# Expert routing of a gated FFN kernel rewritten: ranks from two matmuls, 16-bit one-hots, tile 0 looked up first

## The reference

```python
# layer 1: E = 4, F = 512, VOCAB = 25000, Wg = Wu = Wd = ctx (4, 512, 512)
expert_ids = min(clip(token_ids, 0, VOCAB - 1) // 6250, 3)
for e in range(E):
    g = silu(einsum('bsd,fd->bsf', h, Wg[e]))
    u = einsum('bsd,fd->bsf', h, Wu[e])
    y = einsum('bsf,df->bsd', g * u, Wd[e])
    out = where((expert_ids == e)[..., None], y, out)
# layer 2
g = einsum('th,ih->ti', xf, gate_w) * gate_s
u = einsum('th,ih->ti', xf, up_w) * up_s
out = einsum('ti,hi->th', silu(g) * u, down_w) * down_s
# whole
x = x + tanh(g_xattn[0]) * layer1(layernorm(x))
x = x + tanh(g_ffn[0]) * layer2(layernorm(x))
```

## Time and profile before

| | |
|---|---|
| median of 3 runs | 418.86 us (418.78 to 419.2) |
| the profiled execution, its own time | 418.32 us |
| its span, first to last instruction | 416.5 us |
| busy: PE, DVE, ACT, POOL | 371.1, 249.7, 139.9, 98.7 us |
| mean granted clock of TensorE | 0.991 |
| DMA | 34.53 MB in 14957 packets |

### The profile page before, as it was taken

One profiled execution on the slowest core, in us unless ns is written; L12 is line 12 of the kernel. 1 busy time (PEld: TensorE's weight loads), 2 busy tenths in 40 slices (PEclk: granted clock), 3 DMA queues, 4 the chain that ended last, 5 costly groups with the idle time before them and its releaser, 6 DMA issues.

```text
span 416.5 us, 6049 instructions
## 1 busy us (share of the span) xinstructions
PE 371.1 (89%) x1740; PEld 304.0 (73%) x1740; DVE 249.7 (60%) x461; ACT 139.9 (34%) x240; POOL 98.7 (24%) x135
## 2 busy tenths in 40 slices
PE   0116999999999998999999999999999999999990
PEld 0015788888878876888888888788888888888870
DVE  6998788888887796744545424545425645322243
ACT  4502455454554533633222222322222322222220
POOL 4562445556544232000100200101200101200003
PEclk9999999999999999999999999999999999999996
DMA  7445455655442132530000130000130000100002
GB/s 266 150 133 171 137 146 186 181 169 201 136 170 76 50 127 100 181 126 2 0 2 0 76 126 1 0 0 0 76 126 0 0 0 3 75 23 0 0 2 102
DMA packets 14957, 34.53 MB, mean 83 GB/s; under 512 B 2400, under 2 KB 2400, under 8 KB 14944
## 3 DMA queue, kind: packets, MB, share of 16 engines
q1 hardware_dynamic: 10624, 20.21, 15.2%
q0 software_dynamic: 4320, 14.16, 9.9%
HBM read 25.19 MB, written 9.18 MB: 83 GB/s over the span
## 4 chain that ended last, share of the span: by engine, by line
PE 84%; DVE 9%; POOL 2%; issue 2%; DMA 1%; POOLq 0%; ACT 0%; DVEq 0%
PE bank L1032 38%; PE bank L922 22%; PE bank L1045 19%; PE bank L914 3%; PE bank L936 2%; DVE work L239 1%; DMA rows<-x,gidx 1%; DVE shifted L625 1%; POOL out L442 1%; DVE work L677 1%; DVE is_low L607 1%; POOL rstd L362 1%; DVE is_low L633 1%; DVE xn L650 0%; DMA ids_i<-ids 0%
## 5 line engine op out<-in xcount | busy, mean ns | idle before, releaser
L1032 PE MATMUL bank<-work,wgu 128*128 x704 | 166.8, 389 | 1.3 <-DVE work L677 1.3
L1032 PEld LDWEIGHTS bank<-work,wgu 128*128 128x128 f32 x704 | 132.1, 188 | 29.1 <-issue 1.6
L922 PE MATMUL bank<-work 128*128 x432 | 109.9, 404 | 3.6 <-DVE work L677 2.9
L922 PEld LDWEIGHTS bank<-work 128*128 128x128 f32 x432 | 79.8, 191 | 20.7 <-issue 4.8
L1045 PE MATMUL bank<-work,hp 128*128 128x512 f32 x352 | 88.2, 393 | 0.0
L807 DVE SCALAR_TENSOR_TENSOR sh<-bank,gs,sh 128x512 f32<-128x512 f32 (+1 forms) x45 | 33.1, 738 | 89.3 <-PE bank L1032 89.2
L1045 PEld LDWEIGHTS bank<-work,hp 128*128 128x128 f32 x352 | 65.1, 188 | 13.2 <-DVE hp L812 0.2
L511 ACT ACTIVATE sh<-bank,gs 128x512 f32<-128x512 f32 x44 | 30.3, 689 | 85.4 <-PE bank L1032 84.6
L515 ACT ACTIVATE hp<-sh 128x512 fp32r<-128x512 f32 (+1 forms) x45 | 28.0, 623 | 87.2 <-DVE sh L807 87.2
L812 DVE TENSOR_TENSOR hp<-sh,hp 128x512 fp32r<-128x512 f32 (+1 forms) x45 | 30.6, 680 | 30.1 <-ACT hp L515 30.0
L362 POOL TENSOR_TENSOR rstd<-ve,half 128x1 f32<-128x1 f32 x31 | 17.9, 577 | 128.6 <-DVE ve L644 128.5
(11 more groups left out here) (125 smaller groups left out, 251.4 us busy)
## 6 DMA issues: line engine op xcount, KB each, us to landing
raw<-guT SPq DMA_DIRECT2D x16, 352.0 KB
ctx_in<-ctxT SPq DMA_DIRECT2D x4, 1024.0 KB, 8.9
rows<-x_rows SPq DMA_DIRECT2D x8, 512.0 KB, 4.2
checked<-dwT SPq DMA_DIRECT2D x11, 256.0 KB, 3.0
rows<-dwT SPq DMA_DIRECT2D x11, 256.0 KB, 2.9
dsb<-down_s SPq DMA_DIRECT2D x1, 256.0 KB, 5.0
out<-rows,oidx POOLq DMA_INDIRECT x16, 2.7
rows<-x,inow POOLq DMA_INDIRECT x12, 3.6
```

The source lines that it names most:

```text
L922: mm = pe.matmul(out_ps[:, :], part(s)[:, c * P:(c + 1) * P], ctx_w(e, c, w), start=n == 0, stop=n == last)
L1032: mm = pe.matmul(out_ps[:, :], wgu[:, row + h, w, c * P:(c + 1) * P], moving, start=n == 0, stop=n == last)
```

## The change

- The bounds are compared in one integer operation with a table. The running counts `seen` go to PE as they are, and two accumulated matmul groups give each token's rank and the experts' counts; rounding up to tiles is done by adding a large constant (`ROUND`). The experts' gaps are added in three steps (`slots`).
- The one-hots are 16-bit throughout, with the column index innermost, compared against tables that POOL makes (`minus_j`, `tile_of`). PE looks tile 0 up first, with one column (`token_0`), and its gather starts on a semaphore of its own; the table of the other tiles follows.
- The second lookup goes. Instead POOL scatters the 2048 token numbers by rank into DRAM, sixteen indirect DMAs of 128 words, placed between the gathers, and SP loads `oidx` from there, after the checked rows and ahead of the MLP's first rows.
- All sixteen `ctx_lo` are DVE's. ACT does expert 3's rounding after x_hi(0), and the tanh of the gates after x_hi(1).
- PE waits for the high part before the first pass of a product, for the low part before the second, and in steps 0 to 3 for the weights' rest before the third. Tile 0 always belongs to expert 0.
- The checks stand beside steps 6 to 16, and the maximum follows step 16.

```diff
-POOL_LO = 5
-POOL_LO_NEXT = 7
-POOL_LO_LATE = 14
+ROUND = 1.5 * 2 ** 30
+CHECK_AT = 6
+FIRST = 2
...
+    by_rank = nc.dram_tensor("token_by_rank", [TOKENS, 1], U32).ap()
...
-            sp.wait_ge(S["x_landed"], 16)
...
+            sp.wait_ge(first_landed[FIRST - 1], 16)
             sp.dma_start(dsb[:, :], down_s.partition_broadcast(P)).then_inc(S["small_in"], 16)
-
+            sp.wait_ge(S["x_landed"], 16)
...
+            checks_from = CHECK_AT + RAWS
+            with sp.Fori(RAWS, checks_from) as q:
                 next_piece(q)
-                c, c_before, c_checked = sp.snap(q - 2), sp.snap(16 * (q - 2)), sp.snap(q - 2)
+            with sp.Fori(checks_from, PIECES) as q:
+                next_piece(q)
+                before_q = CHECK_AT + RAWS - 2
+                c, c_before, c_checked = (sp.snap(q - before_q), sp.snap(16 * (q - before_q)),
+                                          sp.snap(q - before_q))
                 sp.wait_ge(S["check_landed"], c_before)
                 hold(sp)
                 sp.wait_ge(S["bits_done"], c_checked)
                 hold(sp)
                 check_row(c)
-            with sp.Fori(RAWS + IC - 2, PIECES) as q:
-                next_piece(q)
-
+            for c in range(2 + PIECES - checks_from, IC):
+                sp.wait_ge(S["check_landed"], 16 * c)
+                sp.wait_ge(S["bits_done"], c)
+                check_row(c)
+            sp.wait_ge(S["ranked"], 16 * CT)
+            sp.dma_start(oidx[:, :], by_rank.rearrange("(t p) o -> p (t o)", p=P),
+                         allow_slow_non_contiguous=True)\
+              .then_inc(S["oidx_ready"], 16)
...
+            pool.iota(minus_j[:, :, :], pattern=[[-1, P], [0, CT]], base=0, channel_multiplier=0, **exact)\
+                .then_inc(S["consts"], 1)
...
+            def place_tokens(c_from, c_to):
+                for c in range(c_from, c_to):
+                    pool.indirect_dma_start(
+                        by_rank, bass.IndirectOffsetOnAxis(ap=rank_i[:, c:c + 1], axis=0),
+                        token_i[:, c:c + 1], None).then_inc(S["ranked"], 16)
...
-            for n in range(POOL_LO):
-                ctx_lo(pool, n)
...
+            pool.wait_ge(S["first_ready"], 1)
+            gather(ring_slot(0), gidx[:, 0:1], first_landed[0])
             pool.wait_ge(S["tables_ready"], 1)
-            for k in range(5):
-                if k:
-                    pool.wait_ge(S["x_landed"], 16 * k)
-                gather(ring_slot(k), gidx[:, k:k + 1])
-                if k == 0:
-                    for n in range(POOL_LO, POOL_LO_NEXT):
-                        ctx_lo(pool, n)
-                if k == 1:
-                    inverse_std(0)
-                if k == 2:
-                    for n in range(POOL_LO_LATE, EXPERTS * KC):
-                        ctx_lo(pool, n)
-                    inverse_std(1)
+            gather(ring_slot(1), gidx[:, 1:2], first_landed[1])
+            gather(ring_slot(2), gidx[:, 2:3])
+            inverse_std(0)
+            pool.wait_ge(S["rank_ready"], 1)
+            place_tokens(0, 2)
+            inverse_std(1)
+            pool.wait_ge(S["x_landed"], 16)
+            gather(ring_slot(3), gidx[:, 3:4])
+            place_tokens(2, 5)
             inverse_std(2)
+            pool.wait_ge(S["x_landed"], 16 * 2)
+            gather(ring_slot(4), gidx[:, 4:5])
+            place_tokens(5, 9)
             inverse_std(3)
-            pool.wait_ge(S["x_landed"], 16 * 5)
+            pool.wait_ge(S["x_landed"], 16 * 3)
             gather(ring_slot(5), gidx[:, 5:6])
+            place_tokens(9, 13)
             pool.wait_ge(S["tables_ready"], 2)
             pool.wait_ge(S["rows_ready"], 1)
             store(ring_slot(0), sidx[:, 0:1])
+            place_tokens(13, CT)
...
+            for e in range(EXPERTS - 1):
+                ctx_hi(e)
             x_hi(0, 0, 0)
+            ctx_hi(EXPERTS - 1)
             silu(0)
             x_hi(1, 0, 0)
+            act.wait_ge(S["small_in"], 16 * 5)
+            act.activation(tg[:, :], gg[:, :], ACT.Tanh).then_inc(S["gates_ready"], 1)
...
-            then(dve.tensor_copy(ids_f[:, :], ids_i[:, :]))
-            for e in range(1, EXPERTS):
-                ins = dve.tensor_scalar(at_least[:, e, :], ids_f[:, :], float(PER_EXPERT * e), None,
-                                        ALU.is_ge)
-            then(ins)
-            then(dve.tensor_tensor(of[:, :, :], at_least[:, 0:EXPERTS, :], at_least[:, 1:EXPERTS + 1, :],
-                                   ALU.subtract))
...
+            then(dve.tensor_tensor(at_least[:, 1:EXPERTS, :],
+                                   ids_i[:, :].unsqueeze(1).to_broadcast([P, EXPERTS - 1, CT]),
+                                   bound[:, :, :], ALU.is_ge))
+            dve.tensor_tensor(of[:, :, :], at_least[:, 0:EXPERTS, :], at_least[:, 1:EXPERTS + 1, :],
+                              ALU.subtract).then_inc(S["route_sb"], 1)
+            dve.wait_ge(S["route_sb"], 1)
+            dve.tensor_tensor_scan(seen[:, 1:], ones_f[:, :], of[:, :, :].rearrange("p e c -> p (e c)"), 0.0,
+                                   ALU.mult, ALU.add).then_inc(S["route_sb"], 1)
...
+            then(dve.tensor_scalar(rounded[:, :], count_up, (P + 1) / 2, ROUND, ALU.max, ALU.add))
+            dve.wait_ge(S["route_pe"], 2)
+            then(dve.tensor_tensor(own_rank[:, :, :], of[:, :, :], bank[3][:, 0:EXPERTS * CT]
+                                   .rearrange("p (e c) -> p e c", e=EXPERTS), ALU.mult))
+            dve.scalar_tensor_tensor(out=gap[:, :], in0=rounded[:, :], scalar=ROUND, in1=count,
+                                     op0=ALU.subtract, op1=ALU.subtract)
+            then(dve.tensor_reduce(rank[:, :], own_rank[:, :, :].rearrange("p e c -> p c e"), AX, ALU.add))
+            before_gap = rank
+            for e in range(EXPERTS - 1):
+                then(dve.scalar_tensor_tensor(out=slots[e][:, :], in0=at_least[:, 1 + e, :],
+                                              scalar=gap[:, e:e + 1], in1=before_gap[:, :],
+                                              op0=ALU.mult, op1=ALU.add))
+                before_gap = slots[e]
+            slot = before_gap
...
+            then(dve.tensor_scalar(tile_up[:, :], slot[:, :], -(P - 1) / 2, ROUND, ALU.add, ALU.add))
+            then(dve.scalar_tensor_tensor(out=minus_low[:, :], in0=tile_up[:, :], scalar=ROUND,
+                                          in1=slot[:, :], op0=ALU.subtract, op1=ALU.subtract))
+            dve.scalar_tensor_tensor(out=token_0[:, :], in0=tile_up[:, :], scalar=ROUND, in1=token[:, :],
+                                     op0=ALU.is_equal, op1=ALU.mult)
+            for h in (slice(0, CT // 2), slice(CT // 2, CT)):
+                dve.tensor_tensor(is_low[:, :, h],
+                                  minus_low[:, h].unsqueeze(1).to_broadcast([P, P, CT // 2]),
+                                  minus_j[:, :, h], ALU.is_equal).then_inc(S["low_ready"], 1)
...
+            then(dve.tensor_tensor(is_high[:, :, :], over_tile(high), tile_of[:, :, :], ALU.is_equal))
+            dve.tensor_tensor_scan(pad_end[:, :], at_least[0:1, 0, 0:EXPERTS], pad[:, :], 0.0,
+                                   ALU.mult, ALU.add)
+            dve.tensor_tensor(in_tile[:, 0, :, :], is_high[:, :, :], over_tile(token), ALU.mult)
+            dve.tensor_tensor(in_tile[:, 1, :, :], is_high[:, :, :], over_tile(rank_up), ALU.mult)\
+               .then_inc(S["route_sb"], 1)
+            dve.wait_ge(S["route_pe"], 3)
+            dve.tensor_copy(gidx[:, 0:1], bank[4][:, 0:1]).then_inc(S["first_ready"], 1)
...
+            dve.tensor_copy(rank_i[:, :], rank[:, :]).then_inc(S["rank_ready"], 1)
...
-            dve.tensor_tensor(is_low[1][:, :, :], per(low[:, 1, :], P), across(P), ALU.is_equal)
-            dve.tensor_tensor(is_high2[:, :, :], per(high[:, 1, :], TILES), across(TILES), ALU.is_equal)\
-               .then_inc(S["route_step"], 1)
...
+            ctx_lo(0, 3)
             landed(0)
             stats(0, ring_slot(0))
-            dve.wait_ge(S["route_step"], steps[0] + 1)
-            dve.tensor_tensor(is_high2[:, :, :], is_high2[:, :, :], per(token[:, :], TILES), ALU.mult)\
-               .then_inc(S["route_sb"], 1)
-            dve.wait_ge(S["ctx_lo"], POOL_LO_NEXT)
+            ctx_lo(3, 4)
             norm(0, ring_slot(0))
-            ctx_lo(dve, 7)
-            ctx_lo(dve, 8)
+            ctx_lo(4, 6)
             x_lo(0, 0, 0)
-            ctx_lo(dve, 9)
-            ctx_lo(dve, 10)
             landed(1)
             stats(1, ring_slot(1))
-            ctx_lo(dve, 11)
+            ctx_lo(6, 7)
             norm(1, ring_slot(1))
-            ctx_lo(dve, 12)
-            ctx_lo(dve, 13)
+            ctx_lo(7, 9)
             hidden(0)
             x_lo(1, 0, 0)
             landed(2)
             stats(2, ring_slot(2))
+            ctx_lo(9, 10)
             dve.wait_ge(S["gates_ready"], 1)
-            with dve.Fori(1, IC + 1) as k:
```

(80 more changed lines are left out.)

228 lines of the change are left out of this document (90 added, 138 removed).

## The result

The kernel takes 433.25 us (median of 4 runs, 430.87 to 434.78), against 418.82 (418.78 to 419.2) before on the same chip: ratio 1.0333, 95% interval 1.03 to 1.0367. It is slower by 14.4 us, and 27 us above the forecast of 406.2.

A forecast was written before the change was run, and what follows sets the result against it. PE was taken to bound the kernel except until the first products and before the MLP; 13.2 + 0.7 − 0.65 − 0.5 = 12.7 us off 418.32 gave 405.6 profiled, 406.2 as median, range 402.6 to 410.6.

The forecast's parts named there:

- Index of tile 0: Routing start: is_low at 5.7 instead of 14.71, 0.65 us a half, first gather issued at 8.7.
- rival D: Routing: the one-hots run at one element a cycle, 1.5 us later, 407.7 us; chance 0.13, inside the forecast's 0.58.
- Landing: Tile 0's gather, meeting the load of ctx_in, lands 5.0 us after issue, at 13.7.
- To first product 1: From tile 0's landing: norm at 16.0, first product 0 at 18.5, first product 1 at 25.1, 15.0 us earlier.
- Steps 1 to 4: First product 1 to 5: 28.7 us against 26.9, scatters priced 1.0 each; first product 5 at 53.8, 13.2 earlier.
- The checks and oidx: Before the MLP: moved checks gain 0.7 and lose 0.65; oidx's load takes 4 us, of which 0.5 reaches PE.
- rival A: Ahead of the MLP: oidx's word-by-word load is slow, 410 us, or 429 at the upper bound; chance 0.16.
- B: Early steps: gathers and scatters hold DVE, eight two-input operations losing 0.5 us each, 410 us; chance 0.08.
- C: Steps 1 to 4 lose nothing, 26.1 us instead of 28.7, 403.6 us in all; chance 0.13.
- E: Slower than before: scatters hold POOL longer than gathers, all sixteen ahead of inverse_std(4); 422 us at 2.0 each; chance 0.04.
- F: Start of the kernel: no change, because ACT or ctx_in bounds it after all; chance 0.01.

The follow-up runs named there:

- Experiment 10: kernel 1 with POOL held by two iotas ahead of the first gather, so that it is issued later; 407.96 us, ratio 0.9736.
- run 3: kernel 1 with an iota holding POOL in place of each of the sixteen scatters, without any DMA; 413.41 us, ratio 0.9864.
- run 7: kernel 1 with sixteen unread scatters to another DRAM tensor, 64 bytes between their 4-byte words; 415.84 us, ratio 0.9924.
- run 2: kernel 1 with the sixteen scatters of neighbouring 4-byte words back in their old places, unread; 430.46 us, ratio 1.0271.
- kernel 1: The changed kernel without the scatters and the load reading them; PE looks oidx up again from 16-bit one-hots; 408.12 us, ratio 0.9734.
- run 12: kernel 1 with expert 3's ctx_in load after tile 0's landing, and the second lookup's one-hots and matmuls moved later; 407.95 us, ratio 0.9724.
- run 9: kernel 1 with seven of the moved two-input subtractions done once more on POOL, around the first gather, unread; 413.48 us, ratio 0.9868.

## Why the prediction was wrong

The working, step by step, in the profiled executions. The forecast's 405.6 was missed by 29.2: 3.0 at first product 1, 19.7 from there to first product 5, 4.5 from there to the MLP (98.0 us, 76.47 to 174.50, where the forecast's terms make 93.5), 1.9 behind it and 0.1 outside the span.

- *Index of tile 0: right to within 0.7.* is_low started at 5.92 (5.7), minus_j was ready at 4.5 (4.2), in time, and the first gather was issued at 9.42 (8.7), 1.07 after the copy of the index started and not 0.47. The halves of is_low took 0.64 each:

```profile
5.92 1.28 DVE L607 TENSOR_TENSOR is_low<-minus_low,minus_j 128x1024 f16<-128x1024 f16 x2
```

  I had 0.65. Mode 2×_1P of the Trainium skill (VectorE: DVE Perf Modes) had made it an estimated 0.70, and 1.2 at one element a cycle: the trace agrees with the rule, and rival D falls.
- *Landing: mis-sized.* 16.0 instead of 13.7, 6.6 after the issue instead of 5.0. I had named tile 0's gather starving behind ctx_in's packets among the things that would make me wrong, and still took a value inside the landings of before (3.2 to 5.3). Experiment 10 shows that an issue 1.7 us later did not matter at all.
- *To first product 1.* From norm on the steps were as forecast: norm at 18.37, first product 0 at 20.77 (2.4 later), which took 7.3 to first product 1 instead of 6.6. 28.08 instead of 25.1.
- *Steps 1 to 4: the step that failed.* "POOL gets sixteen scatters; I price them as a gather, 1.0" counted them on POOL alone, and even there left out the idle of 0.3 between two, whose like stood in brackets in the row I priced them by the earlier trace rows. Of what they do to the DMA engines nothing was said: that term stood at nothing, without a reason. The runs put 5.3 us on POOL's time as the iotas held it (run 3), 7.7 on scatters whose words lie 64 bytes apart (run 7), and 14.6 more on the words being neighbours (run 2 against 7): the two gathers shown above landed 5 and 7 us later than the 3.5 of before. norm(4) waited 6.9 us for rstd, where I had about 1. The idle on PE cost its clock too. The stretch from 46.7 to 62.4 us of after (PE, PEld, DVE, ACT, POOL; clock, DMA share, GB/s):

```profile
46.70:62.40 15.70, 9.59 (x35) 7.47 (x33) 6.76 (x13) 3.35 (x6) 8.15 (x10) 0.67 0.57 102
```

  A mean granted clock of 0.67 lies between the levels of 2.4 and 1.2 GHz; twelve matmuls that took 3.0 took 4.1 to 4.6 around PE's wait of 6.1.
- *Not regained.* I had the steps from 5 on at PE's pace. Of the 4.5 us lost there, 2.1 lie in first product 5 itself. It follows a wait of 4.99 and took 5.07, at a granted clock of 0.58, so that the next matmuls start 5.3 us behind its start and not 3.2 as in kernel 1. The other 2.5 are short waits of PE in the steps behind it. The chain of after shows POOL's own round in them, gather, store, inverse_std, and the wait for the landed store, which the chain gives 3.6 to 5.0 us a time (start, us, what; the first row, 8.16, still lies ahead of first product 5):

```profile
64.63 8.16 DMA x_rows<-rows,inow
75.31 4.61 DMA x_rows<-rows,inow
83.16 3.92 DMA x_rows<-rows,inow
89.61 4.95 DMA x_rows<-rows,inow
...
174.50 7.58 PE bank L1049 x32
```

  The last row is the MLP's first product, at 160.11 before. A round that is as long as a step gives back no delay. That this is where the 2.5 us went is argued from the chain; no run changed it alone.
- *The checks and oidx.* With the scatters out (run 1), 93.5 us pass from first product 5 to the MLP (55.32 to 148.81), against 93.07 before (67.04 to 160.11); my terms without oidx make 93.0. The load of oidx landed in 3.9 us (4 forecast), after:

```profile
L300 SPq DMA_DIRECT2D oidx<-token_by_rank x1: 426/426/426, 153.5 to 153.5; - x1
...
DMA to landing us min/median/max: 3.9/3.9/3.9
```

DVE's timeline where it comes to the MLP's rows:

```profile
161.35 1.28 DVE L666 BATCH_NORM_STATS2 bn<-rows 128x6 f32<-128x512 f32 x2
```

  DVE had no wait ahead of the MLP's rows (no bracket at 161.35, cf.), so its price of 0.5 was 0, and rival A falls. 2048 words read one by one were quick; 2048 words written one by one were not.
- *The rivals.* B: no loss of DVE is to be seen in the steps without scatters, 27.3 us, which is 1.2 above C's 26.1 and 1.4 below my 28.7; with the scatters in, the steps took 48.4 and decide nothing between B and C. E had the sign and the culprit, and a wrong mechanism: a scatter took POOL 1.10 on the mean and 0.30 of idle, not 2.0. By E's own rule (16 × 0.4 us at norm(4)) that is 6.4, and 412.6, near the 413.4 of run 3. The reason that I set against it, that gathers take about 1 whatever they move, holds for POOL's instruction and says nothing of its landing. At 0.04 I priced a risk by one resource only.
- *F.* Fell: the start gained 12.

The rest was right in kind: without the scatters the change gives 10.9 us of the 12.7 forecast. In that kernel's profile first product 1 comes 2.9 later than forecast and the four steps take 1.4 less; the MLP and what follows took 1.3 more than before (257.7 from 148.81 to the end of the span, against 256.4), for which I have no cause.

## What to carry to other kernels

Price an indirect DMA on three accounts: the engine that issues it, its own landing, and what queues behind its packets; a scatter of neighbouring 4-byte words into DRAM looked like any gather on the first (about 1.1 us and 0.3 of idle) and was ruinous on the third, also where nobody waited for it. If words must be scattered, lay them 64 bytes apart (14.6 us here), and better not at all while an idle PE can do the permutation as sixteen one-hot matmuls in 1.2 us, and DVE has 2.3 us of waiting to make the one-hots in. A gather issued beside a large load landed here only when the load was through: split the load, and put what is needed later behind the gather. That brought tile 0 up to 3 us earlier; of it at most 1 us reached the time, which is not clear of the noise.

## What the runs showed of the hardware

- Sixteen scatters of 128 words, by rank into one table of 8 KB, landed after 9.8 us in the median, words 64 bytes apart after 2.6; SP's packets took 0.72 us instead of 0.11 beside the first.
- The gathers' queue had no packet from 9.4 to 13 us, under a load that kept the 16 engines full. With a shorter load (run 12) its packets began between 11 and 12.
- Beside three of DVE's two-input subtractions (10.92 to 12.79) the second gather's instruction ran 2.73 us on POOL instead of 1.0 (the row at 10.89 above). Rival B had asked whether GpSimd would hold DVE; here DVE seems to have held GpSimd. No run tried it alone, and in run 9 a gather that started 0.11 us ahead of three such subtractions took 1.16.
- Beside GpSimd's two-input subtractions, DVE's operations on 19 elements took 1.15 to 1.31 us instead of 0.22 to 0.23 (run 9).
